# A graph network's opening in another order, with 11 turns of the unit matrix around the turn of the edges

## What is computed

```python
h = jnp.maximum(_layernorm(x, axis=-1), 0.0)
q = x @ wq.T + bq
k = x @ wk.T + bk
v = x @ wv.T + bv
q2 = (q @ wiq.T + biq)   # k2, v2 likewise; then masked attention over 16 heads
mask = mask.at[src, dst].set(w[edge_type - 1])
```

## Time and profile before

| | |
|---|---|
| median of 3 runs | 928.07 us (927.96 to 932.13) |
| the profiled execution | 927.87 us, span 926.1 us |
| PE busy | 906.8 us, 98% of the span |
| DVE, ACT, POOL busy | 611.5, 359.2, 492.3 us |
| mean granted TensorE clock | 0.996 |

### The profile page before, as it was taken

How to read it: one execution, slowest core, us unless ns; L and a number is a source line. 1 busy time by engine, 2 the same in 40 slices (tenths; PEclk the granted TensorE clock), 3 DMA queues, 4 the chain that set the end, 5 groups by cost and what they waited for, 6 DMA issues and landing times.

```text
span 926.1 us, 13755 instructions
## 1 busy us (share of the span) xinstructions
PE 906.8 (98%) x4787; PEld 799.0 (86%) x4787; DVE 611.5 (66%) x993; ACT 359.2 (39%) x558; POOL 492.3 (53%) x436
## 2 busy tenths in 40 slices
PE   4999999999999999999999999999999999999998
PEld 4999999998888888888888888888888878888886
DVE  6998888896996735665656565565656565434545
ACT  6433333345885343223223223232325235224422
POOL 5334446775765515757657575756686402220463
PEclk8999999999999999999999999999999999999999
DMA  8998756634336644344554444444333534323412
GB/s 207 241 277 224 229 155 151 167 85 119 53 52 204 178 155 146 92 151 114 152 152 130 153 113 150 113 148 111 97 91 137 182 98 154 114 93 91 140 42 91
DMA packets 89907, 128.60 MB, mean 139 GB/s; under 512 B 34480, under 2 KB 67456, under 8 KB 89856
## 3 DMA queue, kind: packets, MB, share of 16 engines
q1 hardware_dynamic: 72784, 123.54, 43.8%
q0 software_dynamic: 15552, 0.11, 4.0%
q10 hardware_dynamic: 1520, 4.30, 1.4%
HBM read 117.17 MB, written 7.59 MB: 135 GB/s over the span
## 4 chain that ended last, share of the span: by engine, by line
PE 90%; DVE 3%; ACT 2%; POOL 1%; DMA 1%; issue 1%; POOLq 0%; DVEq 0%; ACTq 0%
PE ps L682 49%; PE ps L476 17%; PE ps L756 9%; PE ps L520 4%; PE ps L645 4%; PE ps L600 2%; PE ps L543 2%; PE ps L556 2%; DMA weight_d<-weight_sum,cell 1%; PE ps L435 1%; POOL weight_d L1890 1%; PE ps L892 1%; DVE wlo_all L1388 1%; POOL mean_lo L1869 0%; PE ps L443 0%
## 5 line engine op out<-in xcount | busy, mean ns | idle before, releaser
L1388 DVE TENSOR_TENSOR wlo_all<-raw,whi_all 128x1024 fp32r<-128x1024 f32 x120 | 200.4, 1681 | 119.6 <-ACT whi_all L972 118.5
L476 PE MATMUL ps<-acts,whi_all 128*128 128x384 f32 (+1 forms) x640 | 164.1, 337 | 0.8 <-DVE acts L1400 0.6
L1869 POOL TENSOR_TENSOR mean_lo<-mean_f,mean_hi 128x384 fp32r<-128x384 f32 x76 | 88.3, 1162 | 120.4 <-ACT mean_hi L1124 120.4
L1124 ACT ACTIVATE mean_hi<-mean_f 128x384 fp32r<-128x384 f32 x76 | 39.9, 525 | 277.2 <-DVE mean_f L1562 277.2
L682 PE MATMUL ps<-whi_all,mean_hi 128*128 128x512 f32 x452 | 139.5, 390 | 0.3 <-POOL mean_lo L1869 0.3
L682 PE MATMUL ps<-wlo_all,mean_hi 128*128 128x512 f32 x452 | 139.3, 389 | 0.0
L682 PE MATMUL ps<-whi_all,mean_lo 128*128 128x512 f32 x452 | 139.3, 389 | 0.0
L972 ACT ACTIVATE whi_all<-raw 128x1024 fp32r<-128x1024 f32 x120 | 125.1, 1050 | 32.0 <-PE ps L682 28.5
L476 PEld LDWEIGHTS ps<-acts,whi_all 128*128 128x128 f32 x640 | 116.8, 190 | 1.2 <-DVE acts L1400 0.9
L1890 POOL DMA_INDIRECT weight_d<-weight_sum,cell x48 | 95.5, 1989 | 30.4 <-DMA weight_d<-weight_sum,cell 17.5
L476 PE MATMUL ps<-acts,wlo_all 128*128 128x384 f32 (+1 forms) x320 | 107.6, 336 | 0.0
(11 more groups left out here) (211 smaller groups left out, 1705.6 us busy)
## 6 DMA issues: line engine op xcount, KB each, us to landing
raw<-in_L_gnn_weight SPq DMA_DIRECT2D x64, 512.0 KB
rows_b<-rows_d SPq DMA_DIRECT2D x24, 384.0 KB, 4.8
raw<-in_L_gnn_w_gate SPq DMA_DIRECT2D x16, 512.0 KB
raw<-in_L_gnn_W_self SPq DMA_DIRECT2D x16, 512.0 KB
raw<-in_L_gnn_W_neigh SPq DMA_DIRECT2D x16, 512.0 KB
count_d<-total_r SPq DMA_DIRECT2D x8, 576.0 KB
rel_r<-count_d SPq DMA_DIRECT2D x8, 576.0 KB, 4.5
raw<-in_L_gnn_wq SPq DMA_DIRECT2D x32, 128.0 KB
```

The source lines that it names most:

```text
L476: mm = pe.matmul(ps[:, j % 2, 0:N], stationary[j % RING][:, k, :], acts[:, a, moving, k, :], start=i == 0, stop=i == 3 * KT - 1)
L1124: act.activation(mean_of(q, k, 0)[:, 0, :], sums_of(q, k), ACT.Copy).then_inc(S["mean_hi"], 1)
L1388: dve.tensor_tensor(wlo_row[slot], raw[slot][:, :], whi_row[slot].bitcast(F32), ALU.subtract)\
L1869: pool.tensor_tensor(mean_of(q, k, 1)[:, 0, :], sums_of(q, k), mean_of(q, k, 0)[:, 0, :].bitcast(F32), ALU.subtract).then_inc(S["mean_lo"], 1)
```

## The change

It touches only the first 30 us.

- DVE takes the first two edge keys after the statistics of tile 0, and moves each norm_shift between two half statistics of the next tile. The second pair of edge instructions, now edge_types, comes later, and so do the three small instructions on the edge types' weights, which now stand behind the copy e_col.
- The normalising of node tile 2 (two half tiles) moves from ACT to DVE, without the Relu (start_norm); ACT's copy of those pieces out of PSUM applies the Relu instead, and DVE's subtraction takes a maximum with 0.
- On TensorE the turn of the edges moves behind all turns of h0 and behind the first start_low. Eight turns of the unit matrix stand ahead of it and three behind it (stay_busy); nothing reads what they write.
- The turn of the biases moves from ahead of the first column tile to behind it, and the wait for edge_cols goes with it.
- The edges' DMAs signal in two groups (ends_in for src and dst, edges_in for the types).

SP's instructions are the same 252 rows in the same order, so no load is cut or moved by the change itself.

```diff
             pe.wait_ge(S["ident_made"], 2)
             for n, (nt, k0, k1) in enumerate(START):
-                if n == 2:
-                    turn_edges()
...
-            pe.wait_ge(S["bcol_in"], 16 * 6)
+            def stay_busy(n):
+                for _ in range(n):
+                    pe.transpose(ps[:, 0, 0:P], ident[:, :], ident[:, :])
+            stay_busy(8)
             pe.wait_ge(S["start_lo"], 1)
-            pe.transpose(ps[:, 2, 0:6 * KT], b_in[:, :], ident[0:6 * KT, 0:6 * KT]).then_inc(S["bcol_made"], 1)
-            pe.wait_ge(S["edge_cols"], 1)
+            turn_edges()
+            stay_busy(3)
+            def turn_biases():
+                pe.wait_ge(S["bcol_in"], 16 * 6)
+                pe.wait_ge(S["edge_cols"], 1)
+                pe.transpose(ps[:, 2, 0:6 * KT], b_in[:, :], ident[0:6 * KT, 0:6 * KT]).then_inc(S["bcol_made"], 1)
...
-            eight_tiles(0, 0, ready=turned_at)
+            pe.wait_ge(S["out_lo"], O_CREDIT - 1)
+            column_tile(0, 0, 0, turned_at)
+            turn_biases()
+            eight_tiles(0, 0, first=1)
...
-            start_high(0)
-            norm_std(0, 2)
-            norm_relu_0(*START[2])
-            norm_relu_0(*START[3])
+            norm_std(0, 2)
+            start_high(0)
             tile_high(0, 0)
...
+            def start_norm(nt, k0, k1):
+                dve.wait_ge(S["shift_ready"], nt + 1)
+                dve.tensor_scalar(h0[:, nt, :].rearrange("p (f b i) -> p b f i", f=KT, b=4)[:, :, k0:k1],
+                                  xres[:, nt, :].rearrange("p (b f i) -> p b f i", f=KT, b=4)[:, :, k0:k1],
+                                  rstd[:, nt, :], shift[:, nt, :], ALU.mult, ALU.add).then_inc(S["h_ready"], 1)
...
             turn_tile(0, 0)
+            norm_shift(0, 2)
+            start_norm(*START[2])
+            start_norm(*START[3])
+            edge_types()
             start_low(0)
-            dve.wait_ge(S["edges_turned"], 1)
-            dve.tensor_copy(e_col[:, :, :], ...)
             start_low(1)
             start_low(2)
             start_low(3)
+            dve.wait_ge(S["edges_turned"], 1)
+            dve.tensor_copy(e_col[:, :, :], ...)
+            dve.wait_ge(S["etw_in"], 16)
+            link(dve.tensor_scalar(sp[:, 0, :], etw_b[:, :], 0.0, None, ALU.max))
+            link(dve.tensor_scalar(sp[:, 1, :], etw_b[:, :], -1.0, None, ALU.mult))
+            dve.tensor_tensor(sp[:, 2, :], etw_b[:, :], sp[:, 1, :], ALU.max).then_inc(S["sp_max"], 1)
```

More of the change, by code:

```diff
@@ L940, in start_high @@
                 act.wait_ge(S["start_turned"], n + 1)
-                act.activation(acts[:, 0, 0, k0:k1, P * nt:P * nt + P], start_block(nt, k0, k1), ACT.Copy)\
-                   .then_inc(S["start_hi"], 1)
+                act.activation(acts[:, 0, 0, k0:k1, P * nt:P * nt + P], start_block(nt, k0, k1),
+                               ACT.Copy if nt < NT - 1 else ACT.Relu).then_inc(S["start_hi"], 1)
             HALVES = [slice(0, HALF), slice(HALF, D)]
@@ L1277, in norm_shift @@
                    .then_inc(S["shift_ready"], 1)
[L1279 to L1298, removed]
@@ L1299, in _, with edge_keys @@
-            link(dve.tensor_scalar(sp[:, 1, :], etw_b[:, :], -1.0, None, ALU.mult))
-            dve.tensor_tensor(sp[:, 2, :], etw_b[:, :], sp[:, 1, :], ALU.max).then_inc(S["sp_max"], 1)
+            def edge_keys():
+                dve.wait_ge(S["ends_in"], 16 * 2)
+                dve.scalar_tensor_tensor(e_row[:, KEY, :], e_in[:, 0, :], float(N), e_in[:, 1, :], ALU.mult, ALU.add)\
+                   .then_inc(S["key_made"], 1)
+                dve.scalar_tensor_tensor(e_row[:, KEY_T, :], e_in[:, 1, :], float(N), e_in[:, 0, :], ALU.mult, ALU.add)
@@ L1302, in meet @@
+            dve.wait_ge(x_part[0], 16)
+            half_stats(0, 0)
+            half_stats(0, 1)
+            var_of(0, 0)
+            edge_keys()
+            dve.wait_ge(x_part[1], 16)
+            half_stats(1, 0)
+            norm_shift(0, 0)
+            half_stats(1, 1)
+            var_of(0, 1)
+            dve.wait_ge(x_part[2], 16)
+            half_stats(2, 0)
+            norm_shift(0, 1)
+            half_stats(2, 1)
+            var_of(0, 2)
             def meet(n):
@@ L1354, in start_low @@
                 dve.wait_ge(S["start_hi"], n + 1)
-                dve.tensor_tensor(acts[:, 0, 1, k0:k1, P * nt:P * nt + P], start_block(nt, k0, k1),
-                                  acts[:, 0, 0, k0:k1, P * nt:P * nt + P].bitcast(F32), ALU.subtract)\
-                   .then_inc(S["start_lo"], 1)
+                low, high = [acts[:, 0, a, k0:k1, P * nt:P * nt + P] for a in (1, 0)]
+                if nt < NT - 1:
+                    dve.tensor_tensor(low, start_block(nt, k0, k1), high.bitcast(F32), ALU.subtract)\
+                       .then_inc(S["start_lo"], 1)
+                else:
+                    dve.scalar_tensor_tensor(low, start_block(nt, k0, k1), 0.0, high.bitcast(F32), ALU.max,
+                                             ALU.subtract).then_inc(S["start_lo"], 1)
             dve.wait_ge(S["h_ready"], 1)
             turn_tile(0, 0)
+            norm_shift(0, 2)
+            start_norm(*START[2])
+            start_norm(*START[3])
+            edge_types()
             start_low(0)
-            dve.wait_ge(S["edges_turned"], 1)
-            dve.tensor_copy(e_col[:, :, :], ps[:, 0, 0:4 * EC].rearrange("p (f c) -> p f c", f=4))\
-               .then_inc(S["edge_cols"], 1)
             start_low(1)
```

15 lines of the change are left out of this document (12 added, 3 removed).

## The result

The changed kernel takes 930.38 us (median of 22 runs, 927.79 to 937.34) against 927.98 us before (22 runs, 927.77 to 932.13). The ratio is 1.0031, with a 95% interval of 1.0022 to 1.0040. The forecast was 927.8, so the time is within the range of 926.4 to 931.2, but the sign was not the forecast's: the kernel is slower by 2.4 us in the median, 0.3%, inside the 0.5% to which the prediction gave 0.92.

What follows compares the result with a forecast made beforehand. Bound: DVE's chain through the turn of weight tile 1, then TensorE. That turn at 17.7 instead of 17.99 wins 0.3 us: 927.87 - 0.3 = 927.6, plus 0.2 for the median, 927.8; range 926.4 to 931.2.

Steps and rivals of the forecast that it cites:

- start_norm: DVE's two added normalising instructions: 0.6 us each taken from a subtraction's row, 0.3 us each as the other end.
- the sign: Whole kernel: slightly faster, 0.3 us won on the profiled execution, from 927.87 to 927.6 us.
- The 10.58 us: DVE's chain from the turn of weight tile 1 to column tile 2: work the change leaves alone.
- case C: TensorE's opening: column tiles 0 and 1 hold column tile 2, so quick clock wins 2.2 us, 925.6; chance 0.08.
- SP's edge rows: SP's queue: edge rows stored about 1.5 us later, at 13.5; reload at 19.7 at worst; nothing taken.
- the biases and the Relu on PSUM: ACT's bias copies up to 0.7 us later at slow clock, nothing taken; Relu in PSUM copies and subtractions costs nothing.
- the price of nothing for the pause: TensorE ahead of column tile 2: up to 2.7 us idle, clock holds, so no cost.
- A: The forecast case: TensorE's pause ahead of column tile 2 costs nothing, 927.8 us; chance 0.48.
- B: Slower: clock falls in the pause ahead of column tile 2, costing 1.8 us up to 3.1; chance 0.37.
- the cost of edge_types: DVE ahead of the turn of weight tile 1: the moved edge types counted at 0.4 us.
- the landing of weight tile 0: DVE wants this load at 10.3 rather than 12.4; no row; 0.6 us late makes the gain -0.3 us.
- rival D: Much slower: the clock's fall repeats itself; passing 4.6 us takes 10 us at 0.50; chance 0.03.

Runs made afterwards that it cites:

- e1: The changed kernel without its eleven turns of the unit matrix (both stay_busy calls taken out): 930.37 us, ratio 1.0022 to before.
- e5: The changed kernel with edge_types moved ahead of the turn of weight tile 0: 929.11 us, ratio 1.0000 to before.
- e4: The changed kernel with DVE's turn of weight tile 0 behind start_norm and edge_types, and ACT's copy of it one place later: 930.12 us, ratio 1.0027.
- e2: The kernel before, in its old order, with 8 + 3 turns of the unit matrix added into a free bank: 927.95 us, ratio 1.0004.
- e6: The changed kernel with edge_types early and 16 further unit-matrix turns between column tiles 1 and 2: 927.86 us, ratio 1.0005 to before.
- e3: The changed kernel with 16 further turns of the unit matrix between column tiles 1 and 2: 930.43 us, ratio 1.0017 to before.
- e7: The kernel before with a second, needless cast on DVE ahead of start_low(1), beside POOL's low part: 929.53 us, ratio 1.0012.
- e8: e5 with Exp and Ln earlier, softplus and mask work in DVE's wait, first L1438 ahead of the comparisons: 928.78 us, ratio 1.0009 to before.

## Why the prediction was wrong, and where it was right

**What held.** The end is set by the start of DVE's turn of weight tile 1, and by the clock behind column tile 2. The 10.58 us from that turn to column tile 2 stayed as they were (29.05 - 18.47 in the changed kernel, 30.98 - 20.40 in e1, 28.46 - 17.87 and 29.11 - 18.52 in e5 and e4). A quick column tile 0 brings nothing: before's executions at a mean clock of 1.000 are no faster (e2), and case C did not come. SP's edge rows were stored later, at 14.27, but reloaded at 18.11, as early as before, and the biases and the Relu on PSUM cost nothing that a row shows. In e5's faster executions the forecast is there nearly to the tenth: 927.7 to 927.9, column tile 2 at 28.46, a pause of 2.37 us. Part of that is luck: weight tile 0 is turned 0.8 us later than the working had it (11.07 for 10.3), and DVE's work from there to the turn of weight tile 1 is 0.6 us shorter (6.80 for 7.4), 0.4 of it because e5 moved edge_types away.

**The first step that failed: the price of nothing for the pause (A against B).** The sum took it that TensorE's pause ahead of column tile 2 costs nothing. In the profiled execution the clock fell 1.4 us behind that pause of 2.36 us and cost 1.6 us, the larger part of its 2.0 us. With the cast out of the way (e5), seven of twelve executions still lose about that (929.45 - 927.84 = 1.6, the middles of the two groups); with the pause filled as well (e6), none of the nine below 932 does. In e4 it is six of the nine below 932, and 930.12 - 928.36 = 1.8. So rival B had the mechanism right and the price nearly (1.8 up to 3.1), and its chance of 0.37 was low. The argument against it, 3.20 us at 1.00 without a matmul at the kernel's end, did not carry over: there no work follows that could show a fall, and in the opening the clock stood at 1.00 through the pause and for 1.4 us of work before it fell. The pause itself was sized well (2.36 us, up to 2.7 forecast).

**The second: the cost of edge_types.** The working gave it 0.4 us on DVE, from rows of the kernel before in which the cast took 0.21 us (it stands at 11.56 there, with nothing on POOL beside it). The new place is beside POOL's low part of weight tile 0, and there it takes 2.38 us when it is held (e1), 2.3 more on the chain. The sum counted the work that moved with its old duration, and never asked what the other engine does at the new time. The rows to ask were at hand: POOL is busy 2.20 of the 2.30 us from 14.70 to 17.00, and the prediction's own terms put the two together, ACT's copy of weight tile 0 done at 9.5 + 1.24 + 0.3 + 1.02 + 1.06 = 13.1, edge_types at 8.4 + 1.9 + 1.25 + 0.4 + 1.2 = 13.2. A term of "0.2 or 2.4" was missing. In the changed kernel's profiled execution the cast was not held, so that this loss is in its slower executions too is argued from e1, e3 and e5, not seen.

**The third: the landing of weight tile 0.** The term had no row, and its bound was too narrow. The tile was wanted at 10.3, and at most 0.6 us of lateness was allowed for. DVE was ready at 10.74, since its statistics of node tile 2 started at 8.74 and not 8.4, and the turn started at 11.34, 1.0 us late. A quarter of that was won back, by start_norm (0.50 us each instead of 0.6) and the rest of DVE's work, 7.13 us from turn to turn (7.4 in the working). The chain's start lost 0.48 us where the bound was a loss of 0.3.

**start_norm.** The row of the subtraction gave 0.6, and the estimate by the Trainium skill, "VectorE: DVE Perf Modes", section "Mode 2×_2P — use both read ports for one tensor", about 0.3. Measured: 1.00 us for the two. The measurement decides, and it is nearer to the row.

**Not foreseen and without effect.** The first edge key, 0.23 us before, takes 1.08 us, since it now stands beside POOL's L1824:

```profile
5.79 1.08 DVE L1293 SCALAR_TENSOR_TENSOR e_row<-e_in 48x128 f32<-48x128 int32 x1
```

DVE still waited 0.60 us for weight tile 0 afterwards, so this is hidden in the changed kernel. In e5, where DVE no longer waits there, the chain runs through it.

How the median comes about is not fully shown. The cast is held, by the times, in nine of twelve executions without the turns (930.3 to 930.7, e1). Of the changed kernel's 22 executions one is at 927.8 and nine at 929.4 to 930.1, where the lost clock alone would put them; four lie at 930.3 to 930.8, where the held cast would, though e4 has 930.3 without it. Six at 931.3 to 932.1 are 1 us above either. The two near 937 have mean clocks of 0.993 and 0.994 against 0.998, so about three times as long at half clock, which is rival D in kind. No execution of these last two groups has a profile.

## What to carry to other kernels

When an instruction moves, ask what the other engines do at the new time, GpSimd above all for a cast on VectorE, and not only how long it took at the old one: here a cast of 0.2 us just behind a GpSimd instruction of 2.4 us took 2.4 us, and the same order of the program went either way. TensorE's gain ahead of a wait is no gain; it lengthens the pause, and the clock may fall behind it, in the stretch that sets the end. A median that lies between two groups of times is no size of anything, and two equal medians need not have one cause: sort the executions before fitting a cause, and test one cause at a time.

## What the runs showed of the hardware

- A DVE cast (48x128) started behind a POOL tensor_tensor (128x1024) stood until that ended: 2.38, 2.41 and 2.31 us in e1, e3 and e7, against 0.17 to 0.21 with POOL idle. In the changed kernel's profile it was not held (0.21, with POOL's row 2.74 us long), at the same 0.07 us between the starts as in e1 and e3. An edge key with two inputs beside POOL's AFFINE_SELECT took 1.00 to 1.23 us instead of 0.23 (e4 and e6 the ends).
- DVE's tensor_tensor and scalar_tensor_tensor with one input in PSUM are not held up by the same POOL instruction (e5: 2.35 us for two tensor_tensor, POOL busy 13.49 to 15.90; e4: 1.26 us for two scalar_tensor_tensor, POOL busy 15.49 to 17.86).
- After a pause of 2.2 to 2.5 us behind dense matmuls the granted clock stayed at 1.00 in the profiles of e4 and e5, and went to 0.50 in those of the changed kernel and e8. That one kernel does both is read from its times and mean clocks (e5: five executions at 0.999 or 1.000, seven at 0.997 or 0.998 and 1.6 us slower). Sixteen turns of the unit matrix in the pause left no execution in the group of the fallen clock (e6).
